# Masked attention: the mask for the maxima on VectorE, second scores and exponentials head by head

## What is computed

```python
q, k, v = heads(layernorm(x)) @ Wq.T, heads(ctx) @ Wk.T, heads(ctx) @ Wv.T   # 16 heads of 8
energy = jnp.einsum('nqhd,nkhd->nhqk', q, k)
energy = jnp.where(mask == 0, jnp.float32(-1e+20), energy)
attention = jax.nn.softmax(energy / jnp.sqrt(jnp.float32(EMBED)), axis=3)
out = jnp.einsum('nhql,nlhd->nqhd', attention, v).reshape(n, q_len, EMBED)
x = x + out @ Wo.T + bo
```

## Time and profile before

| what | value |
|---|---|
| median of 3 runs | 1946.27 us (1944.13 to 1948.13) |
| profiled execution, its own time | 1944.69 us |
| its span | 1942.6 us |
| mean granted TensorE clock | 0.901 of full speed |
| busy over the span: PE, weight loads, DVE, ACT, POOL | 1607.9, 1087.6, 1188.3, 814.8, 568.0 us |
| masked layer's first maxima, first second scores, last second scores | 895.8, 914.5, 1077.7 us |

### The profile page before, as it was taken

One profiled execution on the slowest core, in us unless ns is written; L12 is line 12 of the kernel. 1 busy time (PEld: TensorE's weight loads), 2 busy tenths in 40 slices (PEclk: granted clock), 3 DMA queues, 4 the chain that ended last, 5 costly groups with the idle time before them and its releaser, 6 DMA issues. The chain is left out here.

```text
span 1942.6 us, 35018 instructions
## 1 busy us (share of the span) xinstructions
PE 1607.9 (83%) x12418; PEld 1087.6 (56%) x12476; DVE 1188.3 (61%) x4278; ACT 814.8 (42%) x1765; POOL 568.0 (29%) x737
## 2 busy tenths in 40 slices
PE   6796678888789998478888799978867778999888
PEld 4474434555368777454444477745545645677556
DVE  5586454772769996445655233347848875998532
ACT  2342362664248686532545433315643400333422
POOL 2132214310144444216330000032112125777121
PEclk8887878999689998789999889979988978999999
DMA  2000004210257677306220000032110000000000
GB/s 79 12 1 10 30 1 126 57 30 1 72 192 266 230 264 242 136 14 167 60 59 11 18 1 0 1 88 58 47 64 1 1 1 1 3 3 3 1 1 22
DMA packets 81334, 115.16 MB, mean 59 GB/s; under 512 B 8464, under 2 KB 62736, under 8 KB 80400
## 3 DMA queue, kind: packets, MB, share of 16 engines
q0 software_dynamic: 18432, 67.38, 9.8%
q1 hardware_dynamic: 60144, 44.45, 8.3%
q10 hardware_dynamic: 2592, 1.18, 0.3%
HBM read 88.40 MB, written 1.05 MB: 46 GB/s over the span
## 5 line engine op out<-in xcount | busy, mean ns | idle before, releaser
L2758 POOL DMA_INDIRECT f_rows<-tree_table,f_index x128 | 129.0, 1008 | 185.5 <-PE f_ps_y L2959 89.0
L3031 ACT ACTIVATE f_rows<-f_rows,f_low_act 128x128 f32<-128x128 f32 x512 | 152.9, 386 | 0.8
L1782 ACT ACTIVATE x_probs<-x_ps_z 128x768 f32<-128x768 f32 (+1 forms) x128 | 117.3, 917 | 85.6 <-PE x_ps_z L1642 57.6
L2959 PE MATMUL f_ps_y<-f_rows,shared_sb 128*128 128x128 f32 x1024 | 128.3, 288 | 29.2 <-ACT f_rows L3031 29.2
L2959 PEld LDWEIGHTS f_ps_y<-f_rows,shared_sb 128*128 128x128 f32 x1024 | 123.7, 202 | 34.9 <-ACT f_rows L3031 31.6
L82 POOL TENSOR_TENSOR rstd<-moments,shared_sb 128x14 f32<-128x14 f32 (+3 forms) x22 | 4.6, 207 | 471.3 <-DVE moments L66 471.3
L2858 DVE CUSTOM_DVE_ANT_0 f_rows<-f_rows,f_xn 128x128 f32<-128x128 f32 x512 | 111.2, 286 | 22.8 <-DMA f_rows<-tree_table,f_index 22.8
L1472 DVE TENSOR_REDUCE x_minus_max<-x_ps_s 128x4 f32<-128x1024 f32 x64 | 77.8, 1223 | 73.0 <-PE x_ps_s L1642 72.8
L2210 PE MATMUL f_ps_h<-f_xnT,weights 128*128 128x512 f32 x144 | 77.6, 667 | 2.2 <-ACT f_hT L2275 2.2
L2275 ACT ACTIVATE f_hT<-f_ps_h,weights 128x512 f32<-128x512 f32 x72 | 48.6, 685 | 70.4 <-PE f_ps_h L2210 68.6
L2222 PEld LDWEIGHTS f_ps_y<-weights,f_hT 128*128 128x128 f32 x576 | 69.7, 192 | 14.3 <-issue 12.6
(11 more groups left out here) (666 smaller groups left out, 4106.6 us busy)
## 6 DMA issues: line engine op xcount, KB each, us to landing
x_queries<-x_pieces SPq DMA_DIRECT2D x96, 64.0 KB, 2.1
x_keys<-x_pieces SPq DMA_DIRECT2D x84, 64.0 KB, 2.1
a_queries<-a_pieces SPq DMA_DIRECT2D x48, 64.0 KB, 2.1
weights<-w_L_ffn SPq DMA_DIRECT2D x1, 2953.5 KB, 9.6
a_keys<-a_pieces SPq DMA_DIRECT2D x42, 64.0 KB, 2.1
weights<-w_L_ffn SPq DMA_DIRECT2D x1, 2449.0 KB, 9.8
weights<-w_L_ffn SPq DMA_DIRECT2D x1, 2176.0 KB, 9.0
f_rows<-tree_table,f_index POOLq DMA_INDIRECT x128, 6.0
```

What stands on the lines that cost most here:

```text
L1782: a.activation(probs[:, r % HELD, :, :], ps_z[:, :, 0:WIDE], ACT.Exp, scale=scale).then_inc(exped, 1)
L2758: pool.indirect_dma_start(rows[:, place(u, j), tree, :], None, g.tree_table, bass.IndirectOffsetOnAxis(index[:, u % 2, low, j * TREES + tr ...
L2959: last = pe.matmul(ps_y[:, u % SUMS, j, :], g.ident, rows[:, place(u, j), tree, OUT + f * D:OUT + (f + 1) * D], start=False, stop=(low, j, ...
L3031: last = a.activation(row, row, ACT.Copy, scale=low_act[:, u % 3, j * TREES + tree, f:f + 1])
```

## The change

In the masked layer alone (`causal` is None), the first scores get no mask from TensorE. VectorE adds it while it takes the maxima: per head and half of the queries one `tensor_tensor_reduce`, which computes (scores + mask) x -1, writes that to a new tile `hidden` in SBUF and gives the minimum over the 256 keys. It waits for the mask itself, and for its own maxima of the slot before (`hidden` is written again). TensorE makes the second scores of head 0 with their mask, then those of head 1 with theirs, each with a semaphore of its own, and `score` comes behind both. ScalarE takes one exponential per head, and head 0's bank is free after its own. The causal layers keep their instructions.

```diff
--- before.py
+++ after.py
@@ -1301,6 +1301,7 @@
             ident16 = sb("ident16", [P, P], BF16)
             mask_int = sb("mask_int", [P, 2, 2, HALVES, T], I32)
             masks = sb("masks", [P, RINGS, 2, HALVES, T], BF16)
+            hidden = sb("hidden", [P, 2, HALVES, T])
         ps_s, ps_z = ps("ps_s", [P, 2, 2, 512]), ps("ps_z", [P, 2, 512])
         ps_o, ps_p = ps("ps_o", [P, 512]), ps("ps_p", [P, 512])
 
@@ -1313,6 +1314,7 @@
             sem(n) for n in ("tokens_taken", "q_taken", "k_taken", "v_taken", "maxima_taken", "mix_taken", "y_taken"))
         stacked, rows_stored = ([sem(f"{n}{b}") for b in range(of)] for n, of in (("stacked", RINGS), ("rows_stored", 2)))
         scored, max_ready, maxima_made, max_split = (sem(n) for n in ("scored", "max_ready", "maxima_made", "max_split"))
+        first_shifted, first_exped = sem("first_shifted"), sem("first_exped")
         shifted, exped, weighed, sums_ready = sem("shifted"), sem("exped"), sem("weighed"), sem("sums_ready")
         back_made, inverted, mixT_made, y_made, divided, added, stats_taken = (
             sem(n) for n in ("back_made", "inverted", "mixT_made", "y_made", "divided", "added", "stats_taken"))
@@ -1469,8 +1471,14 @@
                     v.tensor_reduce(peaks[:, 0, :], scores[:, :, 0:P], AX.X, ALU.max, negate=True)
                     last = v.tensor_reduce(peaks[:, 1, :], scores[:, :, P:WIDE], AX.X, ALU.max, negate=True)
                 else:
-                    last = v.tensor_reduce(peaks.rearrange("p j h -> p h j"),
-                                           scores.rearrange("p h (j k) -> p h j k", j=HALVES), AX.X, ALU.max, negate=True)
+                    if p == 0:
+                        v.wait_ge(mask_ready, u + 1)
+                    if r >= 1:
+                        v.wait_ge(max_ready, r)
+                    for i in range(2):
+                        for j in range(HALVES):
+                            last = v.tensor_tensor_reduce(hidden[:, i, j, :], scores[:, i, j * T:(j + 1) * T], masks[:, u % RINGS, 0, j, :],
+                                                          -1.0, 3e38, ALU.add, ALU.min, peaks[:, j, i:i + 1])
                 last.then_inc(max_ready, 1)
 
             def split_maxima(u):
@@ -1614,8 +1622,11 @@
                     pe.wait_ge(max_ready, r - 1)
                 for half, out in enumerate((slice(0, P), slice(P, WIDE)) if causal else (slice(0, T), slice(T, WIDE))):
                     for i in range(2):
-                        pe.matmul(ps_s[:, r % 2, i, out], stack_of(queries, u, p, i, half * P, P),
-                                  stack_of(keys, u, p, i, 0, out.stop - out.start), start=half == 0, stop=False)
+                        last = pe.matmul(ps_s[:, r % 2, i, out], stack_of(queries, u, p, i, half * P, P),
+                                         stack_of(keys, u, p, i, 0, out.stop - out.start), start=half == 0,
+                                         stop=half == 1 and not causal)
+                if not causal:
+                    last.then_inc(scored, 1)
 
             def shift(r):
                 u, p = divmod(r, PAIRS)
@@ -1629,18 +1640,27 @@
                         pe.matmul(ps_z[:, i, out], stack_of(keys, u, p, i, half * P, P), stack_of(queries, u, p, i, T - n, n),
                                   start=half == 0, stop=False)
 
+            def shift_by_heads(r):
+                u, p = divmod(r, PAIRS)
+                if p == 0:
+                    pe.wait_ge(rows_stored[u % 2], (u // 2 + 1) * PIECES * 16)
+                    pe.wait_ge(mask_ready, u + 1)
+                for i, (free, made) in enumerate(((first_exped, first_shifted), (exped, shifted))):
+                    if r >= 1:
+                        pe.wait_ge(free, r)
+                    for half in range(HALVES):
+                        pe.matmul(ps_z[:, i, half * T:(half + 1) * T], stack_of(keys, u, p, i, half * P, P),
+                                  stack_of(queries, u, p, i, 0, T), start=half == 0, stop=False)
+                    pe.matmul(ps_z[:, i, :], ident16[:, :], masks[:, u % RINGS, 1, :, :].rearrange("p j k -> p (j k)"),
+                              start=False, stop=True).then_inc(made, 1)
+
             def hide(banks, u, kind):
-                if causal:
-                    for part in range(2):
-                        at = SEEN[kind][part]
-                        for i in range(2):
-                            rows = slice(STACK * i, STACK * (i + 1))
-                            last = pe.matmul(by_parts(banks[:, i, 0:WIDE])[:, :, at], eyes[rows, part, :],
-                                             masks[rows, part, 2 * kind:2 * kind + 2, at], start=False, stop=part == 1)
-                else:
+                for part in range(2):
+                    at = SEEN[kind][part]
                     for i in range(2):
-                        last = pe.matmul(banks[:, i, :], ident16[:, :], masks[:, u % RINGS, kind, :, :].rearrange("p j k -> p (j k)"),
-                                         start=False, stop=True)
+                        rows = slice(STACK * i, STACK * (i + 1))
+                        last = pe.matmul(by_parts(banks[:, i, 0:WIDE])[:, :, at], eyes[rows, part, :],
+                                         masks[rows, part, 2 * kind:2 * kind + 2, at], start=False, stop=part == 1)
                 return last
 
             def weigh(n):
@@ -1695,14 +1715,15 @@
                 if PAIRS <= slot <= BEHIND:
                     fill_wait(pe, g, ps_z[:, 0, :], 512, 5)
                 if pair_at(r) is not None:
-                    shift(r)
+                    if causal:
+                        shift(r)
+                    else:
+                        shift_by_heads(r)
                 if pair_at(slot) is not None:
                     score(slot)
-                if not causal and unit_at(slot) is not None:
-                    pe.wait_ge(mask_ready, unit_at(slot) + 1)
-                if pair_at(r) is not None:
+                if causal and pair_at(r) is not None:
                     hide(ps_z, r // PAIRS, 1).then_inc(shifted, 1)
-                if pair_at(slot) is not None:
+                if causal and pair_at(slot) is not None:
                     hide(ps_s[:, slot % 2, :, :], slot // PAIRS, 0).then_inc(scored, 1)
                 if back_in(r) is not None:
                     turn_back(back_in(r))
@@ -1776,9 +1797,15 @@
                              ps_p[:, 0:T].rearrange("p (n d) -> p n d", d=HD), ACT.Copy).then_inc(v_taken, 1)
 
             def take_probs(r):
-                a.wait_ge(shifted, r + 1)
                 if r >= HELD:
                     a.wait_ge(weighed, (r - HELD) // 2 + 1)
+                if not causal:
+                    a.wait_ge(first_shifted, r + 1)
+                    a.activation(probs[:, r % HELD, 0, :], ps_z[:, 0, :], ACT.Exp, scale=scale).then_inc(first_exped, 1)
+                    a.wait_ge(shifted, r + 1)
+                    a.activation(probs[:, r % HELD, 1, :], ps_z[:, 1, :], ACT.Exp, scale=scale).then_inc(exped, 1)
+                    return
+                a.wait_ge(shifted, r + 1)
                 a.activation(probs[:, r % HELD, :, :], ps_z[:, :, 0:WIDE], ACT.Exp, scale=scale).then_inc(exped, 1)
 
             def take_sums(n):
```

## The result

The change makes the kernel slower: **1957.69 us** median against 1946.27, as the ratio of the runs 1.0039 with the interval 1.0023 to 1.0055. The two don't say the same: 11.4 us between the medians, 7.6 us (4.5 to 10.7) by the ratio. The 17 runs of the changed kernel lie in two groups, five at 1944.6 to 1947.8 us with a mean granted clock of 0.905 to 0.907, and twelve at 1952.6 to 1963.3 us with 0.894 to 0.903; the profiled one is of the second. Why there are two groups is not known. The forecast was 1944.7, "no change", and the time lies 0.7 us beyond the slow end of its range.

The account below looks back on a forecast made before the run. No engine was full; a loop of waits bound the masked layer. Units -0.3, start +0.8 and last slots -2.1 summed to -1.6 us from 1946.3, giving 1944.7 us, "no change", range 1937 to 1957.

Parts of the forecast that it names:

- (a): Masked layer, TensorE: the mask on the first scores goes, two matmuls, 0.44 us a slot.
- (b): VectorE's maxima: four custom instructions with accumulator reads replace one reduction, 0.245 us more; own-maxima wait 0.11, mask wait nothing.
- R: VectorE's time for the maxima of a pair of heads: 1.385 us forecast, bounds 1.14 to 1.96.
- rival A: VectorE's four instructions cost more than the other layer's row: R = 1.67, 11.4 us more, 1956; chance 0.22.
- (c): Second scores by head on TensorE: lost overlap and three more seams make its slot 1.55 us instead of 1.42.
- Rival C: Weights of a head's second half not loaded under the first: 0.18 us more per z, +6.8 us, 1951.5; chance 0.07.
- (d): ScalarE's exponentials by head: 1.02 us becomes 2 x 0.60, and TensorE's 0.47 us wait goes.
- (e): Plain pair of slots: 4.61 us by the chain through VectorE, against TensorE's own 4.32; 4.6 now, so no gain.
- Rival B: Loops looser than chained: weighing doesn't wait for the division, pairs fall to 4.32 us, 7.5 us less, 1937; chance 0.11.
- (f): Units of eight slots: -0.57 us each without projections, +0.5 with them; -0.3 us in all.
- (g): Ends of the masked layer: slots 0 to 7 cost +0.8 us, six pairs in slots 64 to 75 give -2.1 us.
- The term for the clock: Granted clock in the masked layer: 1.00 before; the forecast is wrong if it leaves 1.00 there.

Follow-up runs that it names:

- g3: Changed kernel with only the mask on VectorE, heads together again, old order of waits: 1941.03 us, ratio 0.9963 to the kernel before.
- g1: Changed kernel with the old order of the waits ahead of the exponentials in all three layers: 1953.52 us, ratio 1.0044 to the kernel before.
- n1: Changed kernel with the old order of waits in the masked layer alone: 1957.21 us, ratio 1.0057 to the kernel before.
- k4: Changed kernel with second scores, scores, then masks, old wait order, fillers, first unit's mask and maxima as before: 1930.51 us, ratio 0.9926.
- k5: Changed kernel with scores, both heads' second scores, then masks, old wait order, fillers, first unit's mask and maxima as before: 1922.92 us, ratio 0.9867.
- g2: Kernel before with the two waits ahead of its exponentials exchanged: 1955.42 us, ratio 1.0048 to the kernel before.
- f1: Changed kernel with seven filler matmuls in TensorE's wait ahead of the query projection: 1953.08 us, ratio 1.0045 to the kernel before.
- f4: Changed kernel run again, unchanged: 1957.82 us against 1945.46 for the kernel before, ratio 1.0066.
- n2: Changed kernel with the old order of waits in the causal layers alone: 1952.50 us, ratio 1.0027 to the kernel before.
- k2: Changed kernel with scores, both heads' second scores, then the two masks, old order of waits, fillers: 1924.95 us, ratio 0.9898 to the kernel before.
- f2: Changed kernel with fillers ahead of the query projection and four in each of slots 1 to 7: 1949.32 us, ratio 1.0022.
- g5: Changed kernel with the old order of waits and seven fillers ahead of the query projection: 1948.82 us, ratio 1.0014 to the kernel before.

## Why the prediction was wrong

*The mask leaves TensorE (a).* Right, and worth more than the step said: alone, 5.8 us in the layer (g3).

*VectorE's maxima (b).* Right: 0.345 each, R = 1.39, so rival A is false. The Trainium skill (VectorE: DVE Perf Modes, the section on the TRN2 errata) gives an instruction a fixed 120 cycles from PSUM and 58 from SBUF, 65 ns more at 0.96 GHz, and R = 1.65 is an estimate by it; the trace doesn't show it: 256 columns from PSUM start every 0.345, 128 from SBUF every 0.21, 128 columns more for 0.13. The wait for its own last maxima was mis-sized, 0.23 for 0.11. The accumulator's read is at 912.08, and the next custom instruction starts at 912.31 instead of with it. And "the mask is made ten slots ahead: nothing" missed the second unit, where VectorE stands 0.53 us for it:

```profile
912.08 0.08 DVE L1480 DVE_READ_ACCUMULATOR2_ANT x_minus_max<- 128x1 f32 x1
912.31 0.42 DVE L1480 CUSTOM_DVE_ANT_0 x_hidden<-x_ps_s,x_masks 128x256 f32<-128x256 f32 x1
...
914.30 0.42 DVE L1480 CUSTOM_DVE_ANT_0 x_hidden<-x_ps_s,x_masks 128x256 f32<-128x256 f32 x1 [0.53 <-POOL x_masks L1429]
```

*Second scores by head (c).* The mechanism was right, its size not: a seam is 0.11 at each of five changes instead of 0.10 at four and 0.08 at the fifth, so the slot is 1.61 for 1.55, and the sixth, behind the transposition back, makes that 0.37 for 0.22. Rival C is false as it was put: with the same 64 rows the second load is hidden: the four matmuls of s with their four loads take the same step of 0.32 (1047.41 to 1047.73) as two with two. The Trainium skill (TensorE: Matmul & The Clock Gate, Part 3) says that a load overlaps running matmuls only if its row group differs; the trace shows the load hidden within the same rows and laid open where the number of rows changes.

*Exponentials by head (d).* Right: two passes of 0.60, and TensorE's wait of 0.47 is gone.

*The plain pair (e).* 4.61 forecast, 4.59 to 4.62 measured, with the wrong bound (and the pair of before is 4.78, not the 4.6 that the step read): not the chain through VectorE, but TensorE's own 2 x 1.61 + 0.37 + 1.00 = 4.59, which the step had put at 4.32. Rival B was thus impossible. It could not loosen below TensorE's own time.

*The units (f).* -0.3 forecast. Without the lower clock it is -0.1 (first to 53rd second scores 140.39 in g1 and n1, 140.51 before).

*The ends (g).* Both mis-sized. The start costs 2.0, not 0.8 (20.66 against 18.70 to the first second scores): VectorE's slot is 4 x 0.345 + 0.23 = 1.61 there, and the mask's 0.53 comes on top, so the ninth maxima start 13.55 us behind the first (10.68 before) and end 3.1 us later than before, where the step had 2.5. Of that 1.1 is won back up to the second scores, about as much as the step counted on (half of 2.5 - 0.44): it was the cost that was mis-sized, not the cover. k4 and k5 give 2.2 and 2.0 back with the first unit's mask and maxima as before. The end gives 0.2, not 2.1. The last three pairs take 3.79 for 4.10, near the 3.75 of the step, but they are three and not six. The pair with the output projection takes 4.46 for 4.19, the one ahead of it 4.17 for 4.13, and the half pair at the end 2.50 for 2.08, each by TensorE's longer slot: -0.9 + 0.3 + 0.4 = -0.2. A pair of it in TensorE's timeline after:

```profile
1076.27 0.39 PE L1652 MATMUL x_ps_z<-x_queries,x_keys 64*128 64x256 bf16 x2
...
1080.06 0.39 PE L1652 MATMUL x_ps_z<-x_queries,x_keys 64*128 64x256 bf16 x2
```

So the layer's own sum is +1.6 (185.5 against 183.9) where the forecast had -1.6. That alone would still have been "no change".

**The steps that failed** are two others. "The other two layers of this function keep their instructions; their share is nothing": they keep their instructions and not the order of their waits; 4.1 us, shown in both directions by g1 and g2. And the granted clock was taken to stay at 1.00 in the layer, with the condition that the forecast is wrong if it leaves it; it did, and the layer lost 5.9 us by it: f1 keeps it at 1.00 in the steady part and has 185.5 us, as have g1 and n1, where it did not fall. The term for the clock was put at nothing; what made it fall is open.

1.6 + 5.9 + 4.1 = 11.6, against 11.4 between the first medians. That they meet so closely is luck. The ratio gives 7.6 us and f4's medians 12.4; g1's time lies 5 us above what its layers give, and n2's 5 below. The layers are what is shown.

## What to carry to other kernels

Read a diff for the waits that change places, not only for instructions: put the wait that ends last first, so that the instruction carries it itself, also in callers that the change doesn't mean. On TensorE, count each change of the number of rows in a slot as a cost of its own, and group equal rows before splitting work finer. Run each half of a change alone: here the mask on VectorE was worth 6 us in the layer and the split by heads, as it was built, cost 20. With equal rows together, exponentials by head and fillers, k2 has both halves and gains 20 us. Where the clock may fall behind a wait, try fillers in that wait.

## What was not expected of the hardware

A wait that ends last costs ScalarE 0.06 us more when it stands second in a list of two, in a separate semaphore instruction. A change between 64-row and 128-row matmuls costs TensorE 0.11 us at the upper clock level. And a wait of TensorE doesn't tell by its length, nor by TensorE's work ahead of it, whether the granted clock falls behind it: with the same waits, and the same matmuls in the same places up to where the clock fell, the layer took 185.5 us with the clock at 1.00 in the steady part (g1, n1), 191.4 with two stretches of 6.8 us at 1.2 GHz (after, f4), and 194.3 with three (n2). Filling the wait kept it up each time (f1, f2, g5).
